# Expert tiles that add their gated result straight to the output rows, in a sparse-attention and top-2 expert kernel

## What is computed

```python
x = x + gnn(layernorm(x), adj, Wq, Wk, Wv)              # sparse attention
f = layernorm(x)
probs = softmax(f @ W_router)
topk_p, topk_i = top_k(probs, 2); topk_p /= topk_p.sum(-1)
for e in range(8):
    y = relu(f @ W1[e] + b1[e]) @ W2[e] + b2[e]         # 256 -> 1024 -> 256
    out += combine[:, e:e+1] * y                        # combine: topk_p where e was chosen, else 0
x = x + out
```

## Time and profile before

| | us |
|---|---|
| median of 3 runs (1069.08 to 1070.57) | 1070.33 |
| the profiled execution, its own time | 1069.15 |
| its span, first to last instruction | 1067.5 |
| attention, to 447 | 447 |
| routing and plan, 447 to 565 | 118 |
| expert tiles, 565 to 1014.7 | 449.7 |
| after the last tile, 1014.7 to the end | 52.8 |

### The profile page before, as it was taken

How to read it: one execution, slowest core, us unless ns; L and a number is a source line. 1 busy time by engine, 2 the same in 40 slices (tenths; PEclk the granted TensorE clock), 3 DMA queues, 4 the chain that set the end, 5 groups by cost and what they waited for, 6 DMA issues and landing times.

```text
span 1067.5 us, 23696 instructions
## 1 busy us (share of the span) xinstructions
PE 799.0 (75%) x6721; PEld 731.2 (68%) x6722; DVE 673.1 (63%) x1972; ACT 465.5 (44%) x1309; POOL 440.1 (41%) x440
## 2 busy tenths in 40 slices
PE   2559987997799862254606999999999999999900
PEld 1458876886788751253606988889888898889800
DVE  9867877777688653486275465565565646554555
ACT  2333544343355531143303665655555566565600
POOL 5277777777777732167771000000000000007465
PEclk8578999998899985655557999999999999999955
DMA  9741431422321110222356324241423332124345
GB/s 267 242 109 28 105 103 31 108 71 59 81 51 25 28 31 1 72 86 99 138 182 207 118 74 128 81 141 64 138 79 118 100 116 69 59 79 141 105 144 181
DMA packets 108904, 108.32 MB, mean 101 GB/s; under 512 B 18275, under 2 KB 98100, under 8 KB 108720
## 3 DMA queue, kind: packets, MB, share of 16 engines
q1 hardware_dynamic: 85680, 65.32, 20.1%
q0 software_dynamic: 23168, 42.22, 13.4%
HBM read 93.10 MB, written 40.37 MB: 125 GB/s over the span
## 4 chain that ended last, share of the span: by engine, by line
PE 45%; issue 19%; DVE 15%; POOL 13%; DMA 5%; ACT 2%; DVEq 1%; POOLq 1%; SPq 0%; ACTq 0%
PE psE L1179 10%; POOL nbr L439 7%; PE psH L1168 6%; PE psH L1169 6%; PE psH L1170 6%; PE psE L1181 5%; PE psY L1017 4%; POOL expert_in L486 4%; PE codes L980 2%; DMA xg<-expert_out,gpos 2%; DVE prod L593 2%; PE psQ L1027 1%; PE psX L1155 1%; PE psL L1131 1%; DVE best L575 1%
## 5 line engine op out<-in xcount | busy, mean ns | idle before, releaser
L439 POOL DMA_INDIRECT nbr<-xn_rows,idx x256 | 263.1, 1028 | 108.9 <-issue 104.9
L898 DVE TENSOR_TENSOR h_lo<-z_all,h_hi 128x256 fp32r<-128x256 f32 x296 | 125.2, 423 | 156.4 <-ACT h_hi L1354 156.4
L1353 ACT ACTIVATE z_all<-psH,b1e 128x256 f32<-128x256 f32 x296 | 142.0, 480 | 173.4 <-PE psH L1170 173.4
L1179 PE MATMUL psE<-w_parts,h_hi 128*128 128x512 f32 x552 | 210.2, 407 | 1.7 <-DVE h_lo L898 1.4
L1168 PE MATMUL psH<-x_hi,w_hi 128*128 128x256 f32 (+1 forms) x592 | 167.0, 282 | 13.0 <-issue 6.8
L575 DVE MAX8 best<-codes 128x8 f16<-128x1024 f32 x128 | 150.4, 1222 | 36.4 <-PE codes L980 34.0
L1169 PE MATMUL psH<-x_lo,w_hi 128*128 128x256 f32 (+1 forms) x592 | 167.4, 283 | 0.0
L1170 PE MATMUL psH<-x_hi,w_lo 128*128 128x256 f32 (+1 forms) x592 | 167.0, 282 | 0.0
L1181 PE MATMUL psE<-w_parts,h_lo 128*128 128x256 f32 x552 | 155.4, 281 | 0.0
L1354 ACT ACTIVATE h_hi<-psH,b1e 128x256 fp32r<-128x256 f32 x296 | 141.1, 477 | 0.0
L1017 PEld LDWEIGHTS psY<-diag,nbr 128*128 128x128 f32 x1024 | 133.5, 210 | 7.2 <-issue 4.7
(11 more groups left out here) (258 smaller groups left out, 1096.5 us busy)
## 6 DMA issues: line engine op xcount, KB each, us to landing
adj_in<-in_adj SPq DMA_DIRECT2D x8, 2048.0 KB, 11.1
w_raw<-in_L_ffn_W POOLq DMA_DIRECT2D x16, 1024.0 KB, 5.8
x_in<-expert_in SPq DMA_DIRECT2D x38, 256.0 KB, 2.7
expert_out<-y_out SPq DMA_DIRECT2D x37, 256.0 KB
early_out<-y_out SPq DMA_DIRECT2D x32, 256.0 KB, 2.5
nbr<-xn_rows,idx POOLq DMA_INDIRECT x264, 2.2
x_all<-in_x SPq DMA_DIRECT2D x4, 1024.0 KB, 9.2
xn_rows<-row_all SPq DMA_DIRECT2D x4, 1024.0 KB, 5.0
```

The lines of the kernel that those rows point to most:

```text
L439: pool.indirect_dma_start(nbr[:, u, k, :], None, xn_rows, bass.IndirectOffsetOnAxis(ap=idx[:, u, k:k + 1], axis=0), bounds_check=N - 1, oo ...
L898: dve.tensor_tensor(h_lo[:, hc, :], h_f[:, hc, :], h_hi[:, hc, :].bitcast(F32), ALU.subtract).then_inc(hl_ready, 1)
L1179: pe.matmul(psE[:, q, :], h_hi[:, hc, m], w2_parts[:, b, hc].rearrange("p s c -> p (s c)"), start=(hc == 0), stop=False)
L1353: act.activation(h_f[:, hc, :], psH[:, hc % 4, 0:T], ACT.Relu, bias=b1e[:, b, hc:hc + 1])
```

## The change

The two result tables and the mixing pass at the end are taken out. Instead `out` first gets the rows after the attention (four stores by SP, `store_x2`), and each tile adds to it. `expert_in` and `xg` get four more columns: a token's number (`TOK`), its first expert plus 8 (`FIRST`) and d (`LESS`), so rows are 260 elements (1040 bytes) and each tile carries what it needs. Per tile POOL gathers the present rows of `out` (two indirect DMAs into `acc`), DVE makes y times gate plus `acc` in the middle of the next tile (`add_rows`, at the fifth of the eight steps), and POOL scatters the sum back (two indirect DMAs). At a change of expert POOL's gather waits until the tile before has landed (`after`), since two experts can have the same token.

Besides: the split of the next expert's weights is spread over two tiles, at every second step; SP and not POOL loads the weights, and asks for an expert's third tile of rows between its two matrices; the plan on DVE loses the tile and place tables; the loops over experts on DVE and ACT are written out.

```diff
+TOK, FIRST, LESS = C, C + 1, C + 2
+CX = C + 4
...
             sp.sem_inc(xg_free, 2)
+            sp.wait_ge(attention_done, 1)
+            load_weights(0, 0)
+            load_weights(0, 1)
+            store_x2(0)
+            store_x2(1)
+            load_weights(1, 0)
+            load_weights(1, 1)
             for b in range(2):
                 sp.wait_ge(scattered[b], 32 * QT)
                 sp.sem_inc(xg_free, 1)
+                store_x2(2 + b)
...
+            def load_tile(n, row):
                 wait_alone(sp, x_ps, n + 1)
+                wait_alone(sp, marks_ready, n + 1)
+                wait_alone(sp, less_ready, n + 1)
+                sp.dma_start(x_in[:], expert_in[bass.ds(row, T), :].rearrange("(s p) c -> p s c", p=P)).then_inc(xin_loaded, 16)
...
+                load_tile(before, e * REGION)
+                with sp.If(count > 1):
+                    load_tile(before + 1, e * REGION + T)
+                if weights:
+                    load_weights(e + 2, 0)
+                with sp.If(count > 2):
+                    load_tile(before + 2, e * REGION + 2 * T)
+                if weights:
+                    load_weights(e + 2, 1)
...
+            pool.iota(tok_i[:], pattern=[[P, NT]], base=0, channel_multiplier=1).then_inc(route_consts, 1)
...
+            def rows_of_tile(n, after):
+                wait_alone(pool, marks_ready, n + 2)
+                pool.tensor_copy(tok_next[:], marks[:, :, 0]).then_inc(tok_taken, 1)
+                wait_alone(pool, tok_taken, n + 2)
+                if after:
+                    wait_alone(pool, y_scattered, n * (TS * 16))
+                for q in range(TS):
+                    pool.indirect_dma_start(acc[:, q, :], None, out, bass.IndirectOffsetOnAxis(ap=tok_next[:, q:q + 1], axis=0),
+                                            bounds_check=N - 1, oob_is_err=False).then_inc(acc_ready, 16)
+            def add_tile(done):
+                wait_alone(pool, acc_ready, done * (TS * 16))
+                pool.tensor_copy(tok_now[:], tok_next[:]).then_inc(tok_kept, 1)
+                wait_alone(pool, tok_kept, done)
+                for q in range(TS):
+                    wait_alone(pool, y_ready, done * TS + q + 1)
+                    pool.indirect_dma_start(out, bass.IndirectOffsetOnAxis(ap=tok_now[:, q:q + 1], axis=0), y_out[:, q, :], None,
+                                            bounds_check=N - 1, oob_is_err=False).then_inc(y_scattered, 16)
+            def added(done):
+                wait_alone(pool, y_scattered, done * (TS * 16))
+                pool.sem_inc(y_free, 1)
+            def tiles(e, following):
...
+                with pool.If(count > 1):
+                    with pool.Fori(1, count) as i:
+                        add_tile(before + i)
+                        rows_of_tile(before + i, False)
+                        added(before + i)
+                add_tile(before + count)
+                added(before + count)
+                if following:
+                    rows_of_tile(before + count, True)
...
+                wait_alone(dve, xg_free, q + 1)
+                dve.tensor_copy(xg[:, b, :, TOK].bitcast(I32), tok_i[:, bass.ds(q * QT, QT)])
...
             def rest_of_x(n):
...
+                wait_alone(dve, tok_taken, n + 1)
+                dve.tensor_copy(marks[:], x_in[:, :, TOK:TOK + 2].bitcast(U32)).then_inc(marks_ready, 1)
+            def gate_of(n, e):
+                wait_alone(dve, marks_ready, n + 2)
+                dve.wait_ge(less_ready, n + 2)
+                dve.scalar_tensor_tensor(gate[:, 0], marks[:, :, 1].bitcast(F32), iota_f[:, 0, bass.ds(e, 1)], less_exp[:],
+                                         ALU.is_equal, ALU.max).then_inc(gate_step, 1)
+                dve.tensor_scalar(gate[:, 1], less_exp[:], 1.0, None, ALU.add).then_inc(gate_step, 1)
+                wait_alone(dve, gate_step, n * 4 + 2)
+                dve.reciprocal(gate[:, 2], gate[:, 1]).then_inc(gate_step, 1)
+                wait_alone(dve, gate_step, n * 4 + 3)
+                dve.tensor_tensor(gate[:, 3], gate[:, 0], gate[:, 2], ALU.mult).then_inc(gate_step, 1)
+
+            def add_rows(done):
+                wait_alone(dve, acc_ready, done * (TS * 16))
+                wait_alone(dve, gate_step, done * 4)
+                wait_alone(dve, y_free, done)
+                for q in range(TS):
+                    wait_alone(dve, yo_ready, done * TS + q + 1)
+                    dve.scalar_tensor_tensor(y_out[:, q, :], y_sum[:, q, :], gate[:, 3, q:q + 1], acc[:, q, :],
+                                             ALU.mult, ALU.add).then_inc(y_ready, 1)
+            def tile(n, e, split=None, first=False, alone=None):
                 for hc in range(HC):
+                    if hc == HC // 2:
+                        if not first:
+                            add_rows(n)
+                        gate_of(n, e)
+                    splitting = split is not None and hc % 2 == 1
+                    c = (split or 0) * (SPLITS // 2) + hc // 2
+                    if splitting:
+                        next_weights_hi(e, c)
                     dve.wait_ge(hf_ready, n * HC + hc + 1 + 4)
                     dve.tensor_tensor(h_lo[:, hc, :], h_f[:, hc, :], h_hi[:, hc, :].bitcast(F32), ALU.subtract).then_inc(hl_ready, 1)
+                    if splitting:
+                        next_weights_lo(e, c)
+                if alone is not None:
+                    with dve.If(alone):
+                        for c in range(SPLITS // 2, SPLITS):
+                            next_weights_hi(e, c)
+                            next_weights_lo(e, c)
                 rest_of_x(n + 1)
-                wait_alone(dve, yo_stored, n * 16 + 16)
...
+            add_rows(before + count)
-            dve.wait_ge(lower_fetched, 16 * NT)
...
+                act.activation(less_exp[:], x_in[:, :, LESS], ACT.Exp).then_inc(less_ready, 1)
```

More of the change, by code:

```diff
@@ L207, in attention_and_experts @@
         y_part = sb("y_part", [P, TS, C], F32, ffn)
[L208 to L211 removed]
+        y_sum = sb("y_sum", [P, TS, C], F32, ffn)
+        acc = sb("acc", [P, TS, C], F32, ffn)
+        marks = sb("marks", [P, TS, 2], U32, ffn)
+        tok_now = sb("tok_now", [P, TS], U32, ffn)
+        tok_next = sb("tok_next", [P, TS], U32, ffn)
+        less_exp = sb("less_exp", [P, TS], F32, ffn)
+        gate = sb("gate", [P, 4, TS], F32, ffn)
         ffnp = ExitStack()
@@ L517, in _ @@
+            rows_of_tile(0, False)
+            with pool.Fori(0, E - 1) as e:
+                tiles(e, True)
+            tiles(E - 1, False)
         @block.vector
@@ new lines, in count_of, with before_of @@
+            def count_of(e):
+                return dve.value_load(plan[0:1, 0, e:e + 1], min_val=1, max_val=N // T)
+            def before_of(e):
+                return dve.value_load(plan[0:1, 1, e:e + 1], min_val=e, max_val=MAX_TILES)
+            rest_of_x(0)
+            count, before = count_of(0), 0
+            for e in range(E):
+                last = e + 1 == E
+                tile(before, e, None if last else 0, e == 0, None if last else count < 2)
+                if not last:
+                    next_count, next_before = count_of(e + 1), before_of(e + 1)
@@ L940, in _ @@
-            dve.wait_ge(lower_fetched, 16 * NT)
-            place(0, 0)
-            first = 0
-            for rows in (z_all[:, NT // 2:NT, :], w1_raw[:].rearrange("p k (j c) -> p (k j) c", c=C), w2_raw[:]):
-                groups = rows.shape[1] // GT
-                with dve.Fori(0, groups // 2) as i:
-                    g = i * 2 + first
-                    place(g + 1, 1)
-                    mix(g, 0, lambda u: row(rows, i * (2 * GT) + u))
-                    if first + groups < NG:
-                        place(g + 2, 0)
-                    mix(g + 1, 1, lambda u: row(rows, i * (2 * GT) + (GT + u)))
-                first += groups
+                if not last:
+                    count, before = next_count, next_before
@@ L1359, in attention_and_experts @@
+            count, before = count_of(0), 0
+            for e in range(E):
+                tile_of(before, e)
+                if e + 1 < E:
+                    next_count, next_before = count_of(e + 1), before_of(e + 1)
+                with act.If(count > 1):
+                    with act.Fori(1, count) as i:
+                        tile_of(before + i, e)
+                if e + 1 < E:
+                    count, before = next_count, next_before
     return nc
```

255 lines of the change are left out of this document (78 added, 177 removed).

## The result

The changed kernel takes 1029.37 us (median of 3 runs, 1028.63 to 1029.72) against 1070.33: a ratio of 0.9619, 95% interval 0.9597 to 0.9641. The forecast was 1020. The profiled execution has a span of 1026.7 us and an own time of 1028.63, so its span is 40.8 us shorter than before, where 50.4 was predicted.

What follows compares the result with a forecast made beforehand. TensorE bounds the expert stage, POOL the stages around it. Span 1067.5 - 46.3 (end) - 5 (tiles) + 0.9 (ahead) = 1017.1, own time 1018.75, with 1.18 to the median 1020 us; forecast 1011 to 1028, range 1011 to 1042.

Steps and rivals of the forecast that it cites:

- the second case: Landings at a change of expert at their upper ends, 1036 us, chance 0.26; the range reaches 1042 with slower scatters.
- the first rival: At a change of expert, late landings make the chain 1.6 us late seven times, branches eat 5: 1036; chance 0.26.
- the 5 us in the tiles: Expert tiles: net gain on DVE, 9.2 us less 0.3 for each of 14 weight tiles.
- The end: After the last tile: the gather, add and store stage goes, a shorter one starts earlier; span ends 46.3 us earlier.
- Order on SP ... Cost nothing: SP's queue: tile rows and both weight loads share it; 2.7 and 5.8 us landings fit an 11.89 us tile, cost nothing.
- covered by the tile: Chain through `out` between tiles: 7.85 us within an expert, 9.8 at a change, under 11.89, so cost nothing.
- the prediction's first sign of being wrong: In the tiles: `add_rows` waiting on `acc` or on a landed scatter every tile would show the prediction wrong.
- DVE in the tiles: DVE in expert tiles: added work fits gaps, a weight tile takes 10.8 us, under 11.89; net gain 5 us.
- The 9.2 us: Seven weight-splitting tiles: the excess of 1.31 us in each (13.20 against 11.89) can go, before deductions.
- Ahead of the tiles: Before the first tile: small operations in `route` and at the start add 0.9 us; scatter row length taken as nothing.
- POOL's DMAs held up by DVE: Rival, chance 0.05: POOL's four DMAs per tile at 2.5 us instead of 0.95, 2.2 late each tile, 1098 us.
- The third rival: At the end: landing of `out` rows holds the last tiles back; time stays within 0.2% of 1070; chance 0.03.

Runs made afterwards that it cites:

- the wrong order: Changed kernel with SP issuing both loads of weights ahead of the third tile's rows: 1087.26 us, ratio 1.0156 to the kernel before.
- the loads clear: Changed kernel with each load of weights waiting until the just-issued gathers land, third tile's rows requested ahead of the first load: 1023.75 us, ratio 0.9552.

## Why the prediction was right, and by which steps it was 9 us off

The measured 1029.37 us lie 1.4 above the forecast's own 1011 to 1028. They are inside the stated range because that goes on to the second case, the first rival; and part of that rival is what happened. That the 5 us in the tiles came out near is luck, as shown below.

**The end** was right in kind and mis-sized by 4.7 us. `acc` ends last, as predicted, but 2.93 us after y where 1.8 was put. From POOL's token copy to its first gather, and from DVE's sum to POOL's scatter, the changed kernel has 0.92 us; the prediction took 0.31 for a hand-over from DVE's row, which is no indirect DMA. The other POOL row there, an indirect DMA behind DVE's `pos`, would have been the warning: it starts at 522.92, 0.99 us after `pos` had ended (its 2.12 is POOL's whole idle time). The scatter thus starts 1.40 after DVE's first addition and not 0.75. Landing was right (2.3 for 2.4). The drain of 3.02 us was in no term: in the kernel before it lay under SP's stores, and the chain of waits does not show it. The end of `pos` in the kernel before:

```profile
521.76 0.17 DVE L811 CAST pos<-posq 128x16 uint32<-128x16 f32 x1
```

**"Order on SP ... Cost nothing" is the step that failed**, and with it "covered by the tile" for the chain through `out`. The text looked at what the loads do to SP's own rows, and there it was right (the wrong order costs 58 us). Its sum did not count what the loads do to POOL's gathers, issued at the same moment, since both follow the end of the same tile. It took 2.9 for the landing and 4.4 as the end of the range; a gather under a load took 6.3. So `add_rows` did wait for `acc` in mid-tile, the prediction's first sign of being wrong, though not in every tile. The price is 6.6 us, shown by taking the collision away. The first rival (1036, chance 0.26) named this cause, weights loading at that very time, and half of the place. The rows gathered at a change of expert are added in the middle of the new expert's second tile, which lost 0.51 us to the loads, where the rival put 1.6. The third tiles, whose gathers stand within one expert, lost another 0.64; no text had these.

**DVE in the tiles.** The 9.2 us were about right: the first tiles of experts 1 to 6 fell by 1.57 us on average, 9.4 in all. The deduction of 0.3 for each of 14 weight tiles, for the branch, the reads of the next expert's counts and the catching up, 4.2 in all, was half right. With the loads clear, the second tiles of experts 1 to 6 still take some 0.35 us more than before, 2.1 in all, and DVE's timeline has the reads there; the first tiles show no such loss. So the 5 us came out near the measured 3.2 by errors that cancel in part: 2.1 us less for reads and branches than deducted, a collision of some 6, and 2 us from the place of tiles in memory that nobody had looked for.

**Ahead of the tiles**, +3.9 for +0.9. SP's reads of the plan, and the start of its loop, moved behind the last wait: 1.86 us, shown by taking them off that path. The prediction said that the first tile waits for the last scatter, "nothing", and did not count the instructions that SP now issues between. The scatters take 1.7 us longer in all, seven of them by 0.23 to 0.30 each beside DVE's work on `x_all`; the kernel before has four such, of 1.07 to 1.17. That DVE is the cause is read from the places of the slow ones and was not tried; the same work of DVE stands beside the scatters in the kernel before, so why more of them are slow now stays open. Row length is no large cost: 971 ns median for 961. The first scatter comes 0.5 later, within what executions differ by.

**POOL's DMAs held up by DVE** (0.05, 1098) did not come. By the rule of the Trainium skill that the prediction weighed, SBUF — State Buffer, section "SBUF: two separate sides", POOL's DMAs would have been several times as long; here the trace disagrees in size: the median beside the tiles is 1.046 us for 0.947 without, and the longest scatter of all 1.27. What the trace does show is longer work on DVE beside POOL: of 56 casts of weights in the tiles, 17 run beside one of POOL's indirect DMAs, and 13 of these take 0.58 to 0.68 us; the 39 others take 0.42 at most. One of them, while POOL's scatter runs from 641.33 to 642.36:

```profile
641.91 0.68 DVE L897 CAST w_hi<-w_raw 128x512 fp32r<-128x512 f32 x1
```

The third rival did not come either.

The sum: 3.0 + 1.8 + 4.7 is 9.5 of the 9.6 us that the span missed; the time around it was 1.93 for 1.65, the median 0.74 over the profiled execution for 1.18.

## What to carry to other kernels

When a transfer moves to another queue, ask what else is issued at that moment by anyone, not only what stands behind it in its own queue: two queues released by the same event meet each time. Follow the chain past the last engine row to the closing instructions, and count the register reads between the last wait and the first request. A cover that holds by the median is no cover where a 1 MB load lands at the same time; use the landing under load, or make the load wait.

## What was not expected of the hardware

- Tiles 32 bytes off the 64-byte grid: the first product's matmuls take 280 ns in place of 282 and a plain tile 11.69 us in place of 11.81. Which of the moved tiles does it was not tried.
- A drain of 3.02 us on POOL at the program's end, after its last indirect DMA had landed.
- 0.92 us from the end of the row that POOL waited for to its indirect DMA, against 0.30 from one such DMA to the next.
- Gathers of 128 rows that land in 2.1 us at best take up to 6.3 with 1 MB loads from SP's queue beside them, and 3.8 at most with the loads kept clear.
- Two reads of counts into registers hold SP for 1.2 us and DVE for 1.3.
- DVE's casts of 128x512 take 0.42 us, and mostly 0.66 beside an indirect DMA of POOL.
